# Attention scores as running sums over key differences, maxima bank by bank in the array's two halves, row sums folded by one transfer

## The chip, the cores and the metric

One core of a Trainium2 chip. Its engines are TensorE (PE, with its weight loads as PEld), VectorE (DVE), ScalarE (ACT), GpSimd (POOL) and SyncE (SP), which here issues the transfers. The metric is the device time of one execution in microseconds (us), lower is better.

## The reference

Two transformer layers over x of 32 batch elements x 100 rows x 256. Each adds a gated cross-attention over a context and a gated feed-forward part. The change is in the cross-attention of the second layer (L1): 16 heads, 100 queries, 1444 keys of 64 numbers that serve as values too.

```python
q_big = apply_rope(einsum('bshk,hkq->bshq', q_hk, w_kc_q))      # 192 per head
kv_r  = apply_rope(kv_c, sin_k, cos_k)                          # [32, 1444, 64]
scores = einsum('bhsr,bhlr->bhsl', q_r, k_r)                    # through W_qr, W_kr
attn   = softmax(scores)                                        # over 1444 keys
ctx_c  = einsum('bhsl,bld->bhsd', attn, kv_r)
x = x + tanh(g) * (einsum('bhsd,hkd->bhsk', ctx_c, w_kc_kv) -> [100, 2048]) @ Wo.T
```

The weights between queries and keys are multiplied together ahead, so that a query of a head is 64 numbers (`q1`, in `fp32r`, with its rounding remainder in `q2`), to be multiplied with the 64 of a rotated key (`k1`, with its remainder).

## The kernel before

The phase `phase_l1_attention` goes over 8 groups of 4 batch elements (G = 4). A group has a *head*, which makes the queries of its four elements for all 16 heads (wide matmuls L1431, rotation on DVE L1206 and POOL L1093, absorbed matmuls L1421, copies on ACT L1300), and then the four elements j = 0 to 3. An element has 1600 queries in two chunks of 800 (c = 0, 1, `CQS`); a chunk goes over its 1444 keys in 12 tiles of 121 or 120 keys (`NT`, `KP`). Two key tiles are a pair; the loop over pairs has for each key tile one *slot* (0 to 23 in an element) in which a job from `beside` may stand.

Order on PE in a pair: `scores` of both key tiles (per tile two halves of 400 queries, each half a matmul of `k1` with `q1`, L1476, and one of `k2` with `q2`, L1477, both over 128 rows: `k1` holds the keys rounded above and their remainder below, `q1` the queries twice, `k2` a row of ones and the rounded keys, `q2` the row of negative maxima and the query remainders); the job of the even slot; `values` of the pair before (L1490, exponentials times keys, two column halves); the job of the odd slot. ACT takes the exp of each half (L1350), POOL adds the two tiles of a pair (L1102), DVE adds these to the running sum (L1183, L1186). Scores use four PSUM banks in turn.

The softmax needs the maximum of each query ahead of its scores. `maxima` (L1394) multiplies 128 queries with all 1452 key columns into three banks `m_ps`: three matmuls over rows 0 to 63, 64 to 127 and 0 to 63; the seventh tile of a chunk has 32 queries and uses all 128 rows. DVE reduces the three banks at once (L1163) into `mneg`; PE waits for that before the next tile. SP carries each tile's column into a row of `q2` (L973). There are 14 tiles in an element, one to a job: those of chunk 0 in the element before (in the head for j = 0), those of chunk 1 in the element itself. Other jobs use the same banks: the key transposes (`turn_keys`, L1386), whose results ACT copies (L1306, L1312) and DVE splits (L1157); the sums over partitions (`sums`, L1401) and the output projection (`project`, L1407). The sums go through ACT (L1324), four transfers into `den`, a reciprocal on DVE (L1167), a transfer to HBM and two back into `rdb`, and the normalisation (L1171).

```python
FIRST, LATER, NEXT = (1, 2, 3, 4, 6, 7, 8), (0, 1, 3, 4, 6, 7, 8), (12, 13, 15, 16, 18, 19, 20)
v.tensor_reduce(mneg[0:n, c, t:t + 1], m_ps[0:n, :, 0:4 * KP], AX.XY, ALU.max, negate=True)
```

## Time and profile before

| | |
|---|---|
| median of 3 runs | 3444.43 us (3439.39 to 3446.43) |
| profiled execution | 3444.42 us, its span 3442.4 us |
| granted clock, mean | 0.944 of 2.4 GHz |
| PE busy | 3002.3 us, 87% |
| DVE busy | 2327.0 us, 68% |
| ACT, POOL busy | 1338.1 us (39%), 1559.6 us (45%) |

The span runs from the first to the last instruction. Matmuls overlap and their ends are modelled, so the cost of one is read from start to start. A row of a group gives busy time and mean duration, then the idle time of the engine before its instructions and what ended it.

### The profile page before, as it was taken

The numbers are of one execution on the slowest core, as the hardware profiler recorded it, in microseconds if no ns is written. First come the engines' busy times: TensorE is split into PE (matmuls) and PEld (weight loads), VectorE is DVE, ScalarE is ACT, GpSimd is POOL, SyncE is SP. The second block draws the span as 40 slices with busy tenths as digits, with TensorE's granted clock in tenths as the row PEclk, the third lists the DMA queues.
The fourth block names the chain that finished last, engine by engine and source line by source line (L and its number), as shares of the span: only waits on it lengthen the run. The fifth ranks groups of instructions, "written<-read, shape, count | busy, mean of one in ns | idle before, by whom it ended". The sixth has DMA issues, their size and how long they took to land. (4 is left out here: it accounts for less than half of the span.)

```text
span 3442.4 us, 55921 instructions
## 1 busy us (share of the span) xinstructions
PE 3002.3 (87%) x16656; PEld 2002.3 (58%) x16656; DVE 2327.0 (68%) x3226; ACT 1338.1 (39%) x2810; POOL 1559.6 (45%) x1035
## 2 busy tenths in 40 slices
PE   6999979999699999999999999999999999997344
PEld 4777779999555555565565565555556556554123
DVE  5777754544676676676676667658667667766787
ACT  1323322222244444434434444444443443443456
POOL 0000022222355555555565465556465556553566
PEclk9889979999799999999999999999999999999566
DMA  4000010000200000000000000000000000010100
GB/s 107 0 0 0 0 49 6 10 10 23 59 13 21 17 16 15 22 9 22 15 15 18 20 18 16 19 18 16 15 20 11 22 15 15 10 47 13 60 14 23
DMA packets 130212, 70.65 MB, mean 21 GB/s; under 512 B 83582, under 2 KB 124510, under 8 KB 129880
## 3 DMA queue, kind: packets, MB, share of 16 engines
q1 hardware_dynamic: 129944, 67.45, 7.8%
q8 instruction: 123, 2.02, 0.2%
q14 instruction: 145, 1.19, 0.1%
HBM read 56.95 MB, written 10.04 MB: 19 GB/s over the span
## 5 line engine op out<-in xcount | busy, mean ns | idle before, releaser
L1102 POOL TENSOR_TENSOR c_psum<-c_p 120x800 f32<-120x800 f32 (+1 forms) x384 | 750.8, 1961 | 779.0 <-ACT c_p L1350 463.7
L1163 DVE TENSOR_REDUCE c_mneg<-c_m_ps 128x1 fp32r<-128x1452 f32 (+1 forms) x448 | 744.8, 1662 | 412.6 <-PE c_m_ps L1394 412.4
L1350 ACT ACTIVATE c_p<-c_s_ps 120x400 f32<-120x400 f32 (+1 forms) x1536 | 655.2, 509 | 772.5 <-PE c_s_ps L1477 770.0
L1490 PE MATMUL c_o_ps<-c_p,c_val 120*64 120x400 f32 (+1 forms) x3072 | 598.8, 512 | 5.7 <-DVE c_q L1193 5.7
L1476 PE MATMUL c_s_ps<-c_q,c_k 128*120 128x400 f32 (+1 forms) x1536 | 569.3, 371 | 12.4 <-issue 5.7
L1477 PE MATMUL c_s_ps<-c_q,c_k 128*120 128x400 f32 (+1 forms) x1536 | 529.9, 345 | 0.0
L1394 PE MATMUL c_m_ps<-c_k,c_q 64*128 64x484 f32 (+1 forms) x1344 | 323.9, 439 | 99.9 <-DVE c_mneg L1163 70.8
L1476 PEld LDWEIGHTS c_s_ps<-c_q,c_k 128*120 128x120 f32 (+1 forms) x1536 | 278.9, 182 | 171.6 <-issue 158.8
L1093 POOL TENSOR_TENSOR l_rr<-c_psum,l_rr 96x400 f32<-96x400 f32 x256 | 260.8, 1040 | 210.7 <-DVE l_rr L1206 210.6
L1490 PEld LDWEIGHTS c_o_ps<-c_p,c_val 120*64 120x64 f32 (+1 forms) x3072 | 187.0, 136 | 281.2 <-issue 139.0
L1431 PE MATMUL c_s_ps<-c_xt,l_a 128*96 128x400 f32 x1536 | 309.5, 351 | 1.9 <-DVE c_xt L1151 1.9
L1394 PEld LDWEIGHTS c_m_ps<-c_k,c_q 64*128 64x128 f32 (+1 forms) x1344 | 129.5, 173 | 309.3 <-DVE c_mneg L1163 199.7
L1186 DVE TENSOR_TENSOR c_acc<-c_acc,c_psum 120x800 f32<-120x800 f32 x256 | 279.7, 1092 | 20.8 <-POOL c_psum L1102 18.3
L1431 PEld LDWEIGHTS c_s_ps<-c_xt,l_a 128*96 128x96 f32 x1536 | 240.1, 162 | 79.5 <-issue 41.3
L1477 PEld LDWEIGHTS c_s_ps<-c_q,c_k 128*120 128x120 f32 (+1 forms) x1536 | 280.3, 182 | 2.7
L1300 ACT ACTIVATE c_q<-c_o_ps 64x400 fp32r<-64x400 f32 x256 | 127.7, 499 | 262.6 <-PE c_o_ps L1421 257.9
L528 POOL TENSOR_TENSOR b_act_lo<-b_act,b_act_hi 128x400 fp32r<-128x400 f32 x88 | 91.9, 1049 | 292.4 <-ACT b_act_hi L672 292.4
L717 PE MATMUL b_gu_ps<-b_xt,l_a 128*128 128x400 f32 x1056 | 211.5, 352 | 9.3 <-DVE b_gated L563 9.3
L717 PEld LDWEIGHTS b_gu_ps<-b_xt,l_a 128*128 128x128 f32 x1056 | 193.5, 192 | 13.8 <-DVE b_gated L563 13.7
L1861 PE MATMUL d_y_ps<-d_w,d_hqt 128*128 128x256 bf16 x200 | 43.1, 390 | 110.9 <-ACT d_hqt L1810 110.9
L1206 DVE TENSOR_TENSOR c_psum<-c_s_ps,c_qcos 96x800 f32<-96x800 f32 x128 | 125.8, 983 | 17.8 <-PE c_s_ps L1431 15.6
L734 PE MATMUL b_y_ps<-b_wd,b_act_hi 128*100 128x256 f32 x704 | 129.2, 283 | 0.0
(232 smaller groups left out, 4157.4 us busy)
## 6 DMA issues: line engine op xcount, KB each, us to landing
c_rdb<-l_denominators SPq DMA_DIRECT2D x128, 100.0 KB, 2.7
c_kv<-in_ctx SPq DMA_DIRECT2D x32, 360.0 KB
c_q<-c_mneg SPq DMA_DIRECT2D x384, 0.5 KB, 1.9
c_den<-c_oden SPq DMA_DIRECT2D x256, 0.8 KB
x_rows<-in_x SPq DMA_DIRECT2D x4, 800.0 KB
x_spill<-x_rows SPq DMA_DIRECT2D x8, 400.0 KB
l_xa<-x_spill SPq DMA_DIRECT2D x8, 400.0 KB
c_xr<-x_spill SPq DMA_DIRECT2D x32, 100.0 KB
```

The source lines that it names most:

```text
L717: mm = pe.matmul(gu_ps[:, t % 2, j, 0:T], w[wi][:, k, t * 128:(t + 1) * 128], xt[x][:, k, :], start=(i == 0 and k == 0), stop=(i == 2 and ...
L734: mm = pe.matmul(y_ps[0:S, b // 2, (b % 2) * D:(b % 2 + 1) * D], rows[:, t % RING, b * S:(b + 1) * S], wd[w][:, t, :], start=(t == 0 and b ...
L1093: g.tensor_tensor(rot[:, i % 4, a, :], psum[0:HALF, i % 2, a * T:(a + 1) * T], rs[:, i % 2, (1 - a) * T:(2 - a) * T], ALU.add).then_inc(ro ...
L1102: g.tensor_tensor(psum[0:k, u % 2, :], p[0:k, 2 * u % 4, :], p[0:k, (2 * u + 1) % 4, :], ALU.add).then_inc(psum_ready, 1)
L1163: v.tensor_reduce(mneg[0:n, c, t:t + 1], m_ps[0:n, :, 0:4 * KP], AX.XY, ALU.max, negate=True).then_inc(mneg_ready, 1)
L1186: v.tensor_tensor(acc[0:k, :], acc[0:k, :], psum[0:k, q % 2, :], ALU.add).then_inc(acc_ready, 1)
L1350: a.activation(p[0:k, w % 4, i * HALFQ:(i + 1) * HALFQ], s_ps[0:k, (2 * w + i) % 4, 0:HALFQ], ACT.Exp).then_inc(exp_ready, 1)
L1394: mm = pe.matmul(m_ps[0:n, k, 0:4 * KP], q1[rows, j, c * CQS + t * 128:c * CQS + t * 128 + n], keys[j % 2][rows, k * 4 * KP:(k + 1) * 4 * ...
L1431: mm = pe.matmul(wide_banks(i)[0:HALF, a, 0:T], m.a[w][:, k, HEADS[i], a * HALF:(a + 1) * HALF], xt[x][:, k, :], start=(q == 0 and k == 0) ...
L1476: pe.matmul(o, k1[j % 2][:, r * KP:r * KP + k], q1[:, j, cols], start=True, stop=False)
L1477: mm = pe.matmul(o, k2[j % 2][:, r * KP:r * KP + k], q2[:, j, cols], start=False, stop=True)
L1490: mm = pe.matmul(o_ps[i * DL:(i + 1) * DL, 0:HALFQ], val[0:k, j % 2, r, :], p[0:k, w % 4, i * HALFQ:(i + 1) * HALFQ], start=(r == 0), stop ...
```

## The change

- **Scores.** The four PSUM banks are no longer begun anew for each key tile. Key tile r adds (k_r - k_(r-2)) times the queries onto what the bank holds of tile r - 2. Only tiles 0 and 1 of a chunk start a bank, with the row of negative maxima (`mrow`, against `first`, a row of ones). Queries of the first 400 columns lie in rows 0 to 63 and those of the second 400 in rows 64 to 127, so each matmul covers 64 rows; per key tile there are six, in pairs of the two halves: k1 with q1, k2 (the remainders) with q1, k1 with q2.
- **Keys.** ACT copies the transposed keys once unrounded (`kd`) and once rounded for maxima (`kmax`), DVE rounds the other parts (`round_keys`); POOL takes the differences in place (`difference`, five per element); ACT and DVE round and split them (`round_steps`, nine on ACT, `split_keys`, three on DVE).
- **Maxima.** 13 tiles of 128 queries go over both chunks. Each is three units, one per bank, with a matmul in alternating halves and a DVE reduction of its own (of 484 columns) (`reduce_unit`); seven small reductions per element combine them. In the head the seven tiles keep one reduction over three banks. `UNIT_SLOTS` places 43, 41, 41 and 10 units in the elements j = 0 to 3; the unit's matmul waits for the reduction that last read its bank. In the slots of the key transposes (9, 8, 7) and the one behind them, in slot 3 (j > 0) and in slot 15 there are no units.
- **Sums.** One transfer folds them in place of four, one spreads the inverses in place of two; sums stand in slots 3 and 15, projection in 15, reciprocal and normalisation one pair later.
- **Others.** One exp of a single element ahead of each group; `m.spare` reuses seven semaphores.

```diff
+        m.spare = [a_mm, a_hi, a_out, m_mm, m_out, c_mm, c_out]
...
+    NMT = -(-CH * CQS // 128)
+    NC0 = -(-CQS // 128)
+    starts = [min(128 * t, CH * CQS - 128) for t in range(NMT)]
+    NMU = 3 * NMT
+    NMG = G * NMU
+    COMBINED = {5: (0, 2), 11: (2, 4), 17: (4, 6), 20: (6, 7), 26: (7, 9), 32: (9, 11), 38: (11, 13)}
+    NCB = len(COMBINED)
+    GCB = G * NCB - 4
...
+        kd = sb("c_kd", [DL, NT * KP])
+        kmax = sb("c_kmax", [128, 2, 4 * KP], F32R)
+        klow, khigh = kmax[0:DL], kmax[DL:128]
+        mrow, first = sb("c_mrow", [128, CH, HALFQ], F32R), sb("c_first", [128, KP], F32R)
+        mneg, mpart = sb("c_mneg", [128, NMT], F32R), sb("c_mpart", [128, NMT, 3])
...
+        KEYS = {0: 9, 1: 8, 2: 7}
...
+        def tile_units(tiles):
+            for t in tiles[::2]:
+                yield from ((t, 0, 0), (t, 1, 1), (t, 2, 0))
+                if t + 1 in tiles:
+                    yield from ((t + 1, 1, 1), (t + 1, 0, 0), (t + 1, 2, 1))
+
+        UNITS = [*tile_units(range(NC0)), *tile_units(range(NC0, NMT))]
+        UNIT_SLOTS = ({**dict.fromkeys((1, 2, 3, 4, 5, 6, 11, 12, 13, 14, 16, 17, 18, 19, 20, 22, 23), 2), 7: 3, 8: 3, 21: 3},
+                      {**dict.fromkeys((0, 1, 2, 4, 5, 6, 7, 10, 11, 12, 13, 14, 16, 17, 18, 19, 21, 22, 23), 2), 20: 3},
+                      {**dict.fromkeys((0, 1, 2, 4, 5, 6, 9, 10, 11, 12, 13, 14, 16, 17, 18, 20, 21, 22, 23), 2), 19: 3},
+                      dict.fromkeys((0, 1, 2, 4, 5), 2))
...
+        HEAD_STEPS = {10: (0, 1), 11: (2,), 12: (3,), 13: (4, 5), 15: (6, 7, 8)}
+        TILE_STEPS = {15: (0,), 16: (1,), 17: (2,), 18: (3,), 19: (4,), 20: (5,), 21: (6,), 23: (7,)}
...
+                    sp.dma_start(den[:], oden[0:128:32, :].rearrange("o (p f) -> o p f", p=S // 4)).then_inc(den_loaded, 16)
...
+                    sp.dma_start(rdb[:], io["den"].rearrange("(i n) -> i n", i=2).unsqueeze(1).broadcast_to((2, DL, HALFQ))).then_inc(rdb_loaded, 16)
...
+                def load_tile(t):
+                    for i in range(2 * CH):
+                        lo, hi = max(128 * t, i * HALFQ), min(128 * t + 128, (i + 1) * HALFQ)
+                        if lo < hi:
+                            sp.dma_start(mrow[i % 2 * DL:i % 2 * DL + 1, i // 2, lo - i * HALFQ:hi - i * HALFQ].bitcast(F32),
...
+                                         mneg[lo - starts[t]:hi - starts[t], t:t + 1].bitcast(F32)).then_inc(row_loaded[i // 2], 16)
...
+                def difference(b, r):
+                    if r == NT - 2:
+                        g.wait_ge(kf_ready, PRIMED + (b + 1) * 3)
+                    else:
+                        g.wait_ge(kd_ready, PRIMED + b * 5 + (NT - 2 - r) // 2)
+                    g.sem_inc(m.carrier, 1)
+                    new, old = slice(r * KP, (r + 2) * KP), slice((r - 2) * KP, r * KP)
+                    g.tensor_tensor(kd[:, new], kd[:, new], kd[:, old], ALU.subtract).then_inc(kd_ready, 1)
...
+                        if j + 1 < G and at in (5, 6):
+                            for r in ((10, 8, 6), (4, 2))[at - 5]:
+                                difference(b + 1, r)
...
+                def round_keys(b):
+                    v.wait_ge(kf_ready, PRIMED + b * 3 + 1)
+                    v.tensor_copy(klow[:, 0, :], m_ps[0:DL, 0, 0:4 * KP]).then_inc(kmax_low, 1)
+                    v.wait_ge(kmax_high, PRIMED + b * 2 + 2)
+                    v.tensor_copy(klow[:, 1, :], m_ps[0:DL, 2, 0:4 * KP]).then_inc(kmax_low, 1)
+
+                def split_keys(b, j, pieces):
+                    for k in pieces:
                         cols = slice(k * 4 * KP, (k + 1) * 4 * KP)
-                        v.wait_ge(k1_hi, PRIMED + b * 3 + k + 1)
-                        v.tensor_tensor(k1[j % 2][DL:128, cols], m_ps[0:DL, k, 0:4 * KP], k1[j % 2][0:DL, cols].bitcast(F32),
+                        v.wait_ge(k1_hi, PRIMED + b * 6 + k + 1)
+                        v.sem_inc(m.carrier, 1)
+                        v.tensor_tensor(k2[j % 2][0:DL, cols], kd[:, cols], k1[j % 2][0:DL, cols].bitcast(F32),
                                         ALU.subtract).then_inc(k1_ready, 1)
 
-                def reduce_max(ch, c, t):
-                    n = QT[t]
-                    v.wait_ge(maxs_ready, PRIMED + ch * NQT + t + 1)
-                    v.tensor_reduce(mneg[0:n, c, t:t + 1], m_ps[0:n, :, 0:4 * KP], AX.XY, ALU.max, negate=True).then_inc(mneg_ready, 1)
+                def reduce_tile(gi, t):
+                    v.wait_ge(maxs_ready, PRIMED + gi * NMG + 3 * t + 3)
+                    v.tensor_reduce(mneg[:, t:t + 1], m_ps[:, :, 0:4 * KP], AX.XY, ALU.max, negate=True).then_inc(mpart_ready, 3)
+
+                def reduce_unit(it, n):
+                    t, bank, half = UNITS[n % NMU]
+                    v.wait_ge(maxs_ready, PRIMED + it * NMG + n + 1)
+                    v.tensor_reduce(mpart[:, t, bank:bank + 1], m_ps[:, bank, 0:4 * KP], AX.X, ALU.max, negate=True).then_inc(mpart_ready, 1)
+                    if n % NMU in COMBINED:
+                        tiles = slice(*COMBINED[n % NMU])
+                        v.wait_ge(mpart_ready, PRIMED + it * NMG + n + 1)
+                        v.tensor_reduce(mneg[:, tiles], mpart[:, tiles, :], AX.X, ALU.min).then_inc(mneg_ready, 1)
...
+                        if (j, c) != (0, 0) and q == 5:
+                            normalise(ch - 1, 1 - c)
+                        if j + 1 < G and c == 1 and q >= 3:
+                            split_keys(it * G + j + 1, j + 1, [q - 3])
...
+                def copy_keys(b):
                     for k in range(3):
                         a.wait_ge(kt_ready, PRIMED + b * 3 + k + 1)
-                        a.activation(k1[j % 2][0:DL, k * 4 * KP:(k + 1) * 4 * KP], m_ps[0:DL, k, 0:4 * KP], ACT.Copy).then_inc(k1_hi, 1)
-
-                def place_keys(b, j, k):
-                    cols = slice(k * 4 * KP, (k + 1) * 4 * KP)
-                    a.wait_ge(k1_hi, PRIMED + b * 3 + k + 1)
-                    a.sem_inc(m.carrier, 1)
-                    a.activation(k2[j % 2][DL:128, cols], k1[j % 2][0:DL, cols].bitcast(F32), ACT.Copy).then_inc(k2_ready, 1)
+                        a.activation(kd[:, k * 4 * KP:(k + 1) * 4 * KP], m_ps[0:DL, k, 0:4 * KP], ACT.Copy).then_inc(kf_ready, 1)
+                        if k > 0:
+                            a.activation(khigh[:, k - 1, :], m_ps[0:DL, k, 0:4 * KP], ACT.Copy).then_inc(kmax_high, 1)
+
+                def round_steps(b, j, n):
+                    cols = slice(n % 3 * 4 * KP, (n % 3 + 1) * 4 * KP)
+                    if n < 6:
+                        a.wait_ge(kd_ready, PRIMED + (b + 1) * 5)
+                        a.sem_inc(m.carrier, 1)
+                        a.activation(k1[j % 2][n // 3 * DL:(n // 3 + 1) * DL, cols], kd[:, cols], ACT.Copy).then_inc(k1_hi, 1)
+                    else:
+                        a.wait_ge(k1_ready, PRIMED + b * 3 + n - 5)
+                        a.sem_inc(m.carrier, 1)
+                        a.activation(k2[j % 2][DL:128, cols], k2[j % 2][0:DL, cols].bitcast(F32), ACT.Copy).then_inc(k2_ready, 1)
...
+                    a.activation(warm[:], m.ident[0:1, 0:1], ACT.Exp)
...
+                def maxima_unit(it, n):
+                    j, k = divmod(n, NMU)
+                    t, bank, half = UNITS[k]
+                    rows, q = slice(half * DL, (half + 1) * DL), slice(starts[t], starts[t] + 128)
...
+                    pe.wait_ge(mpart_ready, PRIMED + it * NMG + last_in(bank, n) + 1)
+                    pe.matmul(m_ps[:, bank, 0:4 * KP], q1[rows, j, q], kmax[rows, bank // 2 if half == 0 else bank - 1, :],
+                              start=True, stop=True).then_inc(maxs_ready, 1)
...
+                        bank = [s_ps[:, (2 * w + i) % 4, 0:HALFQ] for i in range(2)]
+                        if (j, c) == (0, 0) and r < 2:
+                            pe.wait_ge(roped, PRIMED + 2 * (it * H + H - 1 + r))
+                        if w >= 2:
+                            pe.wait_ge(exp_ready, PRIMED + 2 * it * NU + 2 * w - 2)
...
+                        if r < 2:
+                            for i in range(2):
+                                pe.matmul(bank[i][0:KP], first[side[i], :], mrow[side[i], c, :], start=True, stop=False, skip_group_check=True)
                         for i in range(2):
-                            at = 2 * w + i
-                            if at >= 4:
-                                pe.wait_ge(exp_ready, PRIMED + 2 * it * NU + at - 3)
-                            cols = slice(c * CQS + i * HALFQ, c * CQS + (i + 1) * HALFQ)
-                            o = s_ps[0:k, at % 4, 0:HALFQ]
-                            pe.matmul(o, k1[j % 2][:, r * KP:r * KP + k], q1[:, j, cols], start=True, stop=False)
-                            mm = pe.matmul(o, k2[j % 2][:, r * KP:r * KP + k], q2[:, j, cols], start=False, stop=True)
-                            mm.then_inc(s_ready, 1)
+                            pe.matmul(bank[i][0:k], k1[j % 2][side[i], keys], q1[side[i], j, q[i]], start=False, stop=False, skip_group_check=True)
+                        for i in range(2):
+                            pe.matmul(bank[i][0:k], k2[j % 2][side[i], keys], q1[side[i], j, q[i]], start=False, stop=False, skip_group_check=True)
+                        for i in range(2):
+                            pe.matmul(bank[i][0:k], k1[j % 2][side[i], keys], q2[side[i], j, c, :], start=False, stop=True, skip_group_check=True).then_inc(s_ready, 1)
```

## Rows read from the trace of the kernel before

**Rows 1.** The page: busy time of each engine, and TensorE's granted clock in 40 slices.
```profile
PE 3002.3 (87%) x16656; PEld 2002.3 (58%) x16656; DVE 2327.0 (68%) x3226; ACT 1338.1 (39%) x2810; POOL 1559.6 (45%) x1035
...
PEclk9889979999799999999999999999999999999566
```

**Rows 2.** Busy time by stretch: one group's head, elements 0, 1 and 3.
```profile
core 0: us, PE busy (x) PEld busy (x) DVE busy (x) ACT busy (x) POOL busy (x), PEclk, DMA share, GB/s
2037.28:2097.83 60.55, 57.92 (x307) 39.33 (x306) 53.09 (x60) 17.89 (x36) 33.65 (x33) 1.00 0.03 5
2097.83:2153.01 55.18, 49.47 (x254) 27.63 (x255) 36.99 (x30) 27.68 (x61) 29.42 (x17) 1.00 0.10 24
2153.01:2211.08 58.07, 53.26 (x279) 30.45 (x279) 37.66 (x32) 25.38 (x58) 31.11 (x18) 1.00 0.08 18
...
2269.10:2319.27 50.17, 49.07 (x263) 28.53 (x261) 30.00 (x39) 22.03 (x52) 34.09 (x19) 1.00 0.09 21
```

**Rows 3.** Timeline of PE, one engine, in the second half of an element.
```profile
start us, us, engine line op out<-in xcount [idle before <-releaser]
...
2002.05 0.70 PE L1394 MATMUL c_m_ps<-c_k,c_q 64*128 64x484 f32 x3
2002.68 1.56 PE L1490 MATMUL c_o_ps<-c_p,c_val 120*64 120x400 f32 x8
...
2007.08 0.84 PE L1394 MATMUL c_m_ps<-c_k,c_q 128*32 128x484 f32 x3 [0.22 <-DVE c_mneg L1163]
2007.85 1.56 PE L1490 MATMUL c_o_ps<-c_p,c_val 120*64 120x400 f32 x8
2009.34 0.45 PE L1476 MATMUL c_s_ps<-c_q,c_k 128*120 128x400 f32 x1
2009.63 0.35 PE L1477 MATMUL c_s_ps<-c_q,c_k 128*120 128x400 f32 x1
...
2011.00 1.56 PE L1490 MATMUL c_o_ps<-c_p,c_val 120*64 120x400 f32 x8
2012.49 3.70 PE L1407 MATMUL c_m_ps<-l_cvo,c_ct 128*100 128x256 f32 x16
2015.84 0.53 PE L1476 MATMUL c_s_ps<-c_q,c_k 128*121 128x400 f32 x1
...
2020.70 0.55 PE L1401 MATMUL c_m_ps<-c_acc,c_ones 121*32 121x200 f32 x8
2021.18 1.56 PE L1490 MATMUL c_o_ps<-c_p,c_val 121*64 121x400 f32 x8
```

**Rows 4.** Timeline of PE and its loads, 2157.110 to 2157.118; one block of loads.
```profile
2157.11 0.49 PE L1394 MATMUL c_m_ps<-c_k,c_q 64*128 64x484 f32 x2 [0.27 <-DVE c_mneg L1163]
...
2157.11 0.19 PEld L1394 LDWEIGHTS c_m_ps<-c_k,c_q 64*128 64x128 f32 x2 [0.96 <-DVE c_mneg L1163]
...
2004.51 0.30 PEld L1394 LDWEIGHTS c_m_ps<-c_k,c_q 64*128 64x128 f32 x3 [0.96 <-DVE c_mneg L1163]
```

**Rows 5.** Timeline of DVE in the stretch of element 1.
```profile
2155.39 1.67 DVE L1163 TENSOR_REDUCE c_mneg<-c_m_ps 128x1 fp32r<-128x1452 f32 x1 [2.55 <-PE c_m_ps L1394]
2156.97 0.98 DVE L1186 TENSOR_TENSOR c_acc<-c_acc,c_psum 120x800 f32<-120x800 f32 x1
2157.87 1.66 DVE L1163 TENSOR_REDUCE c_mneg<-c_m_ps 128x1 fp32r<-128x1452 f32 x1
...
2167.35 0.20 DVE L1167 RECIPROCAL c_rden<-c_den 100x8 f32<-100x8 f32 x1
...
2172.81 1.66 DVE L1171 TENSOR_TENSOR c_ct<-c_onum,c_rdb 128x400 f32<-128x400 f32 x1
```

**Rows 6.** Groups by line in the stretch of element 1: DVE, ACT, POOL.
```profile
L1157 DVE TENSOR_TENSOR c_k<-c_m_ps,c_k 64x484 fp32r<-64x484 f32 x3 | 1.8, 647 | 0.5 <-ACT c_k L1306 0.5
...
L1350 ACT ACTIVATE c_p<-c_s_ps 120x400 f32<-120x400 f32 (+1 forms) x48 | 20.5, 509 | 26.4 <-PE c_s_ps L1477 26.3
...
L1312 ACT ACTIVATE c_k<-c_k 64x484 fp32r<-64x484 f32 x3 | 1.8, 604 | 0.1
...
L1102 POOL TENSOR_TENSOR c_psum<-c_p 120x800 f32<-120x800 f32 (+1 forms) x13 | 25.9, 1997 | 30.0 <-ACT c_p L1350 16.3 <-DVE c_acc L1186 13.7
```

**Rows 7.** Timeline of PE: the first score matmul of element 1.
```profile
2153.01 0.44 PE L1476 MATMUL c_s_ps<-c_q,c_k 128*121 128x400 f32 x1 [0.68 <-DMA c_q<-c_mneg]
```

More of the change, by code:

```diff
@@ new lines, in units_at, with last_in, first_in @@
+        def units_at(j, slot):
+            first = 3 * NC0 + sum(sum(UNIT_SLOTS[i].values()) for i in range(j)) + sum(n for s, n in UNIT_SLOTS[j].items() if s < slot)
+            return range(first, first + UNIT_SLOTS[j].get(slot, 0))
+        assert units_at(G - 1, CT).start == NMG
+        assert all(units_at(j, KEYS[j]).start == NMU * (j + 1) for j in KEYS)
+        def last_in(bank, n):
+            return next(i for i in range(n - 1, -1, -1) if UNITS[i % NMU][1] == bank)
+        def first_in(bank, n):
+            return next(i for i in range(n, n + NMU) if UNITS[i % NMU][1] == bank)
@@ L938, in _ @@
             def _(sp):
+                for c in m.spare:
+                    sp.sem_clear(c)
                 for c in counters:
@@ L1533, in group @@
+                        for n in units_at(j, slot):
+                            maxima_unit(it, n)
                     for u, j, c, q in pairs():
@@ L1572, in count @@
         def count(name):
-            counters.append(sem(name))
+            counters.append(m.spare.pop() if m.spare else sem(name))
             return counters[-1]
```

283 lines of the change are left out of this document (149 added, 134 removed).

## Prediction

> **What bounds the kernel now.** I began with the page: TensorE (PE) is busy 87% of the span, VectorE (DVE) 68%, and PE's clock is granted at its upper level (2.4 GHz) nearly everywhere [rows 1]. All edits but a list of spare semaphores lie in the attention of the second layer, which fills some 2256 us (8 x 282.0, below). I cut one of its eight groups into its head and its four batch elements, each stretch from its first matmul to that of the next [rows 2] (the fourth is not shown; it repeats the third in 58.0 us). The five take 60.6, 55.2, 58.1, 58.0 and 50.2 us, 282.0 together, and the groups repeat this within half a microsecond. The reader is to see that in the heads DVE is busy 53 of 60.6 us, and in the elements PE 49 to 53 us, DVE 30 to 38.
>
> What an element costs PE is read from start to start in the timeline, since the ends are modelled [rows 3]. A pair of key tiles has a block of 8 score matmuls, 1.66 us from its start to that of what follows: 8 x 0.183, and 0.19 for entering and leaving (the first interval is 0.28, the later ones 0.18). The values take 1.49, a maximum of one query tile 0.63 (0.77 for the 32-row tile), the output projection 3.35, the sums 0.48, the key transposes about 1.2. For the third stretch: 12 x (1.66 + 1.49) + 12 x 0.63 + 2 x 0.77 + 3.35 + 2 x 0.48 + 1.2 = 52.4. It takes 58.1: 5.7 us are waits, nearly all for the maximum on DVE, before the next tile may overwrite the three banks. The same sum gives 50.1, 52.4 and 47.4 for the other three, so waits of 5.1, 5.6 and 2.8.
>
> **The change, part by part.**
>
> *Scores.* Four matmuls per key tile over 128 rows become six over 64 rows, three in each half of the array, issued in pairs with different halves and banks. What a pair costs is shown by the maxima, whose first two matmuls are such a pair: both loads and both matmuls start inside one window of 8 ns [rows 4], and the block of three takes 0.63, where three over 128 rows take 0.77 [rows 3]. So I price a pair like one matmul, 0.183. A block falls to 6 x 0.183 + 0.19 = 1.29. The two blocks of an element in which a chunk begins have two pairs more for the row of maxima, +0.37 each. So 12 x 1.29 + 0.74 = 16.2 us where 12 x 1.66 = 19.9 stood. The trace does not show pair after pair, so both ends: below, 0.183 (the same 400 columns stream); then 0.21, if the two loads of a pair take turns (the first interval shows a load of 120 columns uncovered for 0.10); then 0.283, if no load is covered; above, 0.366, if the halves take turns. I take the lower end, because the row with two starts is the same form of matmul.
>
> *A rule weighed.* In the maxima the third load belongs to the half in which the first matmul still streams, and the three loads are over 0.30 us after the block began [rows 4]: a load and a matmul of one half do overlap. The Trainium skill (TensorE: Matmul & The Clock Gate, Part 3) says that a weight load overlaps a running matmul only when its row group differs. By that rule each pair would start 0.10 later and the time would be 3377; by the row it is 3233.
>
> *Maxima.* Instead of 14 blocks of three matmuls there are 39 single ones per element, two or three to a slot, halves alternating, so a slot costs PE one step of 0.22 (0.63 less the 0.19, halved) and no entry, as the scores beside it use the same halves. Stretch by stretch (43, 41, 41 and 10 units): 23, 21, 21 and 5 steps, 5.2, 4.7, 4.7 and 1.1 us.
>
> PE's floor: third and fourth stretch 16.2 + 17.9 + 4.7 + 3.35 + 0.96 + 1.2 = 44.3; second 16.2 + 17.9 + 5.2 + 0.5 + 1.2 + 1.5 (the last query pair) = 42.5; fifth 16.2 + 17.9 + 1.1 + 3.35 + 0.96 + 0.7 (turning rows) = 40.2.
>
> *DVE.* Its maximum over 1452 elements takes 1.58 from start to start, the sum over 800 takes 0.90 [rows 5]. That is 1.04 ns per element, so 484 elements take 0.57, and three of them 1.71 instead of 1.58. Bounds: 0.50 (the slope alone) and 0.65 (the busy time of the form with 484 columns [rows 6]). Third stretch: 41 x 0.57 = 23.4; seven small minima that each wait for the maximum just issued, 0.25 each (nearest row the reciprocal, 0.20 [rows 5], and a lost overlap), 1.8; twelve running sums 11.5; two normalisations 2.1; reciprocals and residual 0.6; two copies of keys 1.1; three subtractions 1.9. Together 42.4, beside PE's 44.3.
>
> These don't simply overlap. PE can be ahead by three banks only, and gives DVE no maxima in slots 8, 9, 3 and 15. DVE then runs dry: around the projection PE spends 1.49 + 0.48 + 3.35 + 1.29 = 6.6 us between two slots, for which DVE has 2.5 (4.1 idle); around the other sums 3.3 for 2.1 (1.1 idle); around the keys 5.6 for 3.2 (2.4 idle). 42.4 + 7.6 = 50.0. In the dense slots between, four maxima and a running sum are 3.2 to 3.5 us of DVE, with key subtractions and normalisations up to 4.3, against PE's 1.29 + 1.49 + 0.44 = 3.2: there DVE leads. With 1 us for a bank that comes round after two units, 51.0 for the third and fourth stretch. Second: 43.1 us of DVE, 5.5 idle: 49.0. Fifth: PE's 40.2, and 3 for the backlog and the chunk's row: 43.0.
>
> *Head.* Seven tiles keep the wide maximum. DVE gets two key copies and keeps three subtractions, two operations more, +1.1: 61.6. The exp of one element placed ahead of the group takes a table load off ACT; I count nothing, as PE there has other work.
>
> *ACT and GpSimd (POOL).* ACT gets 8 more copies of 484 columns per element, 0.56 to 0.60 each, some 4.8 us, hidden by the 26 us in which it waits for scores [rows 6]; uncovered they would cost 150 us. POOL gets five subtractions over 242 columns, from 2.00 us for 800 some 0.6 each, 3 us, in 30 us of waits [rows 6]; with them its share rises, and DVE's operations without PSUM may stretch, as the normalisation did that took 1.66 us [rows 5]. For that I put 0 to 2 us per element into the range.
>
> *Transfers.* SP issues 16 row pieces instead of 14, one fold instead of four, one spread instead of two. They lie beside PE work except the row before an element's first score, 0.68 us late at 2153.01 [rows 7]. In the second stretch it is reduced later (slot 21), 1 us, which is in the waits.
>
> **Sum.** 61.6 + 49.0 + 51.0 + 51.0 + 43.0 = 255.6, less than 282.0 by 26.4; x 8 = 211. The profiled execution took 3444.42 us (span 3442.4), equal to the median of the runs. 3444.4 - 211 = 3233.
>
> **Rivals.**
>
> *PE sets the pace.* If DVE's units cost 0.50 and its sequences interleave well, each element stands 2 us above its floor: 61.6 + 44.5 + 46.3 + 46.3 + 42 = 240.7, x 8 = -330, 3114. Against it: DVE then still has 39 us of work and 7 of holes. 0.10.
>
> *DVE costs more.* Units at 0.65 (135 per group outside the head, x 0.08 = 11) and 1 to 2 us per element from POOL: 255.6 + 15 = 271, 3356; or ACT's copies hold up the exponentials with the like result. 0.15.
>
> *Loads uncovered.* Pair interval 0.283: floors rise by 12 x 6.2 x 0.1 = 7.4 to 50 to 52 us, PE leads, with 3 us of waits 61.6 + 53 + 55 + 55 + 49 = 273.6: 3377. 0.06.
>
> *The halves take turns (the other side).* Interval 0.366: a score block costs 12 x 0.183 + 0.19 = 2.39, the maxima 0.22 a unit; floors 61 to 64, fifth 56, group about 308: 3444 + 8 x 26 = 3652. With waits of 3 us per element over the floors the group comes to 282 at an interval of about 0.31; from there on the change loses. Against it are the two starts in 8 ns; for it, that they don't accumulate and that no second pair follows. 0.06.
>
> *No net change* within 0.2% (7 us, about what a measurement of this kernel can tell): interval near 0.30. 0.01.
>
> **Chances.** Forecast 0.62, the others as above: faster 0.93, same 0.01, slower 0.06. Range 3150 to 3340: from between the first rival and the forecast (two thirds of DVE's lower bound) to most of the second.
>
> **What would show it.** The 12 matmuls of two key tiles should stand in six steps of 0.18, pairs a few ns apart. The DVE rows of 484 elements should be 0.65 busy, 0.57 apart. PE's waits should be for them in slots 16 to 23 and before the key transposes. The stretches should read 62, 49, 51, 51, 43. Wrong would be: pairs further apart than 0.2, exponentials waiting on ACT's copies or POOL, a row that arrives late by several us, or a lower granted clock.

## The result, and the profile after

The kernel after takes 3499.36 us, the median of 4 runs (3484.78 to 3511.37), beside 3445.43 (3439.39 to 3449.17) for the one before on the same chip. The ratio is 1.0156, 95% interval 1.0112 to 1.0201: slower by 54 us, where 3233, 211 us faster, was forecast. The profiled execution took 3511.37 us (span 3509.6, mean clock 0.911 where it had been 0.944).

From the page of the kernel after: span, busy times, granted clock and two groups of DVE (busy and mean, then idle before and releaser).

```profile
span 3509.6 us, 61563 instructions
...
PE 2942.7 (84%) x18344; PEld 1971.0 (56%) x18352; DVE 2449.7 (70%) x4170; ACT 1488.0 (42%) x3074; POOL 1640.1 (47%) x1196
...
PEclk9888879999899998999999999899999999998566
...
L1283 DVE TENSOR_TENSOR c_acc<-c_acc,c_psum 120x800 f32<-120x800 f32 x256 | 322.4, 1259 | 63.8 <-POOL c_psum L1178 61.8
...
L1268 DVE TENSOR_TENSOR c_ct<-c_onum,c_rdb 128x400 f32<-128x400 f32 x64 | 37.4, 585 | 153.4 <-DMA c_rdb<-l_denominators 153.3
```

PE is busy for 59.6 us less than before [rows 1], with 1,688 matmuls more: the scores did get cheaper. But its share of the span fell from 87 to 84%, and the normalisation of DVE waited 153.3 us for the transfer `c_rdb`, the spread of the inverses.

The same cut of a group as in [rows 2], now with all five stretches (head, then elements 0 to 3), of the kernel after:

```profile
core 0: us, PE busy (x) PEld busy (x) DVE busy (x) ACT busy (x) POOL busy (x), PEclk, DMA share, GB/s
2071.00:2134.60 63.60, 58.32 (x309) 39.36 (x307) 54.44 (x63) 23.49 (x45) 36.24 (x38) 1.00 0.04 9
2134.60:2185.60 51.00, 46.60 (x315) 26.37 (x317) 40.19 (x65) 30.66 (x69) 34.27 (x22) 0.97 0.10 21
2185.60:2250.30 64.70, 53.39 (x335) 30.86 (x333) 43.66 (x69) 30.24 (x66) 33.58 (x22) 0.89 0.10 16
2250.30:2311.30 61.00, 52.92 (x337) 30.43 (x333) 40.24 (x69) 30.34 (x66) 33.82 (x22) 0.92 0.10 18
2311.30:2361.00 49.70, 45.04 (x307) 25.08 (x307) 33.00 (x48) 22.54 (x53) 31.74 (x19) 0.97 0.12 22
sum 290.00, PE 256.27 PEld 152.09 DVE 211.52 ACT 137.27 POOL 169.65; mean PE 51.25 PEld 30.42 DVE 42.30 ACT 27.45 POOL 33.93
```

Forecast were 61.6, 49, 51, 51 and 43, together 255.6. It is 290.0, 34.4 more, and 8 x 34.4 = 275 of the 278 us by which the profiled execution missed. Element 0, with one normalisation where the others have two, is 2 us over; elements 1 and 2 are 13.7 and 10.0 over, at a clock of 0.89 and 0.92, and element 3 is 6.7 over.

The largest single loss, from the timeline of the kernel after at the start of element 1 (SP's issues are SPq; the bracket is the idle time of the engine and what ended it):

```profile
2183.30 0.52 SPq L1005 DMA_DIRECT2D l_denominators<-c_rden  x1
...
2184.81 0.58 SPq L1010 DMA_DIRECT2D c_rdb<-l_denominators  x1
...
2192.04 0.58 DVE L1268 TENSOR_TENSOR c_ct<-c_onum,c_rdb 128x400 f32<-128x400 f32 x1 [5.28 <-DMA c_rdb<-l_denominators]
2192.53 0.65 DVE L1246 TENSOR_TENSOR c_k<-c_kd,c_k 64x484 fp32r<-64x484 f32 x1
2193.10 1.22 DVE L1256 TENSOR_REDUCE c_mpart<-c_m_ps 128x1 f32<-128x484 f32 x2
...
2193.80 0.85 PE L1530 MATMUL c_m_ps<-c_kmax,c_q 64*128 64x484 f32 x2 [5.08 <-DVE c_mpart L1256]
...
2194.35 0.16 DVE L1260 TENSOR_REDUCE c_mneg<-c_mpart 128x2 fp32r<-128x6 f32 x1
2194.56 0.99 DVE L1283 TENSOR_TENSOR c_acc<-c_acc,c_psum 120x800 f32<-120x800 f32 x1
```

In the program the normalisation stands ahead of the next maxima, and DVE takes them in that order: it begins the normalisation 7.2 us after the spread was issued and the maxima behind it, at 2193.10. Until then PE has no bank for its next maxima and idles for 5.08 us. In the kernel before, the transfers of the same place were issued at 2168.89, and the normalisation began at 2172.81 without idle time, right behind a maximum [rows 5].

PE then pays a second time, by its clock. Windows of the kernel after, same columns as above:

```profile
2185.50:2188.00 2.50, 2.50 (x24) 1.81 (x24) 1.25 (x3) 1.60 (x4) 0.00 (x0) 1.00 0.14 32
2188.00:2193.50 5.50, 0.72 (x6) 0.03 (x2) 1.46 (x3) 0.09 (x1) 0.00 (x0) 0.85 0.08 26
2193.50:2199.50 6.00, 5.70 (x24) 3.52 (x24) 4.34 (x8) 2.91 (x6) 3.77 (x3) 0.57 0.03 2
2199.50:2205.00 5.50, 5.31 (x47) 3.25 (x45) 3.35 (x6) 2.87 (x8) 4.33 (x3) 1.00 0.01 0
```

At work again, PE runs 6 us at a granted clock of 0.57, most of them at its lower level (1.2 of 2.4 GHz): 24 matmuls, of mixed forms, in 6.0 us, and 47 in the next 5.5. Such a wait of 5.2 to 5.7 us comes once in each of the eight groups, and in all eight the 6 us from the normalisation on show a clock of 0.50 to 0.52. The other waits of the stage are at most 3.5 us. In the heads DVE waits 3.2 to 3.4 us for the same transfer, but PE has work meanwhile and its clock stays 1.00. In element 2 DVE waits 1.9 and 2.7 us for it, PE is idle for 2.1 and 2.4, and the clock falls to 0.57 and 0.50 again. Over the whole attention stage the clock is 0.95, where it was 1.00 before. The waiting line of `c_rdb` names the first loss only: over the stage PE is busy for 2033.6 of 2316 us here and for 1975.1 of 2178 us in the kernel of experiment 1, with the same matmuls. So some 58 of the 138 us between the two stages are the same work done more slowly, an estimate from these busy times.

The score blocks themselves did what was forecast. PE's timeline of the kernel after, a block of two key tiles:

```profile
2199.98 0.44 PE L1619 MATMUL c_s_ps<-c_q,c_k 64*120 64x400 f32 x2
2200.26 0.34 PE L1621 MATMUL c_s_ps<-c_q,c_k 64*120 64x400 f32 x2
2200.44 0.34 PE L1623 MATMUL c_s_ps<-c_q,c_k 64*120 64x400 f32 x2
2200.63 0.34 PE L1619 MATMUL c_s_ps<-c_q,c_k 64*120 64x400 f32 x2
2200.81 0.35 PE L1621 MATMUL c_s_ps<-c_q,c_k 64*120 64x400 f32 x2
2200.99 0.35 PE L1623 MATMUL c_s_ps<-c_q,c_k 64*120 64x400 f32 x2
2201.17 0.38 PE L1530 MATMUL c_m_ps<-c_kmax,c_q 64*128 64x484 f32 x2
```

What counts are the starts: twelve matmuls stand in six steps of 0.18, the first a little longer, and the block takes 1.19 to the maxima behind it.

### The profile page after: what moved, and what is told of

It is laid out like the page before. It is cut to its first block and busy times, and to the rows that moved or that the text cites. A ratio compares the mean times of both kernels' runs of the same rounds, so it can differ in the third digit from the quotient of the medians.

```text
span 3509.6 us, 61563 instructions
## 1 busy us (share of the span) xinstructions
PE 2942.7 (84%) x18344; PEld 1971.0 (56%) x18352; DVE 2449.7 (70%) x4170; ACT 1488.0 (42%) x3074; POOL 1640.1 (47%) x1196
## 5 line engine op out<-in xcount | busy, mean ns | idle before, releaser
L1256 DVE TENSOR_REDUCE c_mpart<-c_m_ps 128x1 f32<-128x484 f32 x1080 | 656.5, 651 | 164.5 <-PE c_m_ps L1530 159.9
L1635 PE MATMUL c_o_ps<-c_p,c_val 120*64 120x400 f32 (+1 forms) x3072 | 629.2, 533 | 27.5 <-ACT c_onum L1429 16.3
L1530 PE MATMUL c_m_ps<-c_kmax,c_q 64*128 64x484 f32 x1080 | 340.8, 471 | 174.1 <-DVE c_mpart L1256 170.3
L1530 PEld LDWEIGHTS c_m_ps<-c_kmax,c_q 64*128 64x128 f32 x1080 | 153.2, 194 | 405.8 <-DVE c_mpart L1256 329.4
L1283 DVE TENSOR_TENSOR c_acc<-c_acc,c_psum 120x800 f32<-120x800 f32 x256 | 322.4, 1259 | 63.8 <-POOL c_psum L1178 61.8
L1635 PEld LDWEIGHTS c_o_ps<-c_p,c_val 120*64 120x64 f32 (+1 forms) x3072 | 194.4, 141 | 292.4 <-issue 170.1
L1619 PE MATMUL c_s_ps<-c_q,c_k 64*120 64x400 f32 (+1 forms) x1536 | 319.8, 375 | 2.3 <-ACT c_p L1462 2.3
L1623 PE MATMUL c_s_ps<-c_q,c_k 64*120 64x400 f32 (+1 forms) x1536 | 302.9, 355 | 0.0
L1621 PE MATMUL c_s_ps<-c_q,c_k 64*120 64x400 f32 (+1 forms) x1536 | 302.6, 355 | 0.0
L1619 PEld LDWEIGHTS c_s_ps<-c_q,c_k 64*120 64x120 f32 (+1 forms) x1536 | 165.0, 188 | 60.6 <-issue 32.1
L1621 PEld LDWEIGHTS c_s_ps<-c_q,c_k 64*120 64x120 f32 (+1 forms) x1536 | 172.3, 188 | 4.8
L1623 PEld LDWEIGHTS c_s_ps<-c_q,c_k 64*120 64x120 f32 (+1 forms) x1536 | 172.7, 188 | 0.9
L1268 DVE TENSOR_TENSOR c_ct<-c_onum,c_rdb 128x400 f32<-128x400 f32 x64 | 37.4, 585 | 153.4 <-DMA c_rdb<-l_denominators 153.3
```

Of the source, the lines that this page charges most:

```text
L1256: v.tensor_reduce(mpart[:, t, bank:bank + 1], m_ps[:, bank, 0:4 * KP], AX.X, ALU.max, negate=True).then_inc(mpart_ready, 1)
L1283: v.tensor_tensor(acc[0:k, :], acc[0:k, :], psum[0:k, q % 2, :], ALU.add).then_inc(acc_ready, 1)
L1530: pe.matmul(m_ps[:, bank, 0:4 * KP], q1[rows, j, q], kmax[rows, bank // 2 if half == 0 else bank - 1, :], start=True, stop=True).then_inc( ...
L1619: pe.matmul(bank[i][0:k], k1[j % 2][side[i], keys], q1[side[i], j, q[i]], start=False, stop=False, skip_group_check=True)
L1621: pe.matmul(bank[i][0:k], k2[j % 2][side[i], keys], q1[side[i], j, q[i]], start=False, stop=False, skip_group_check=True)
L1623: pe.matmul(bank[i][0:k], k1[j % 2][side[i], keys], q2[side[i], j, c, :], start=False, stop=True, skip_group_check=True).then_inc(s_ready, 1)
```

## The experiments

**1. Two transfers instead of one.** The kernel after with the spread of the kernel before:

```diff
-  sp.dma_start(rdb[:], io["den"].rearrange("(i n) -> i n", i=2).unsqueeze(1).broadcast_to((2, DL, HALFQ)))
+  for i in range(2):
+      sp.dma_start(rdb[i * DL:(i + 1) * DL, :], io["den"][i * HALFQ:(i + 1) * HALFQ].partition_broadcast(DL))
```

> The changed kernel with one edit undone: the inverses go back to all partitions by two transfers of 64 partitions, not by one of 128. Theory A (the one wide transfer lands 7.2 us after its issue, the two of before 2.7 us after; DVE stands at the normalisation for it, the maxima queue behind, PE idles and its clock falls): DVE's wait for this transfer falls from 153 us to under 40 us, the third and fourth stretch of a group from 65 and 60.5 us to about 57 and 55, the total to 3330 to 3390. Rival B (the order on SP's queue makes the transfer late, not its shape): the landing falls but the wait stays over 100 us, total over 3450. Rival C (DVE's maxima in single units and the paired matmuls are too dear): no change, 3480 or more.

3367.28 us (3361.0 to 3370.97), ratio to the kernel before 0.9773 (0.9741 to 0.9804): the sign of the whole change turns on this line. The same stretches of this kernel:

```profile
2004.50:2066.40 61.90, 58.17 (x309) 39.24 (x307) 55.71 (x63) 23.83 (x46) 36.59 (x38) 1.00 0.03 6
2066.40:2117.30 50.90, 45.20 (x312) 25.72 (x312) 40.31 (x64) 30.45 (x67) 34.06 (x22) 1.00 0.09 21
2117.30:2174.60 57.30, 49.10 (x335) 28.32 (x335) 43.61 (x69) 29.92 (x66) 33.70 (x22) 1.00 0.10 20
2174.60:2229.00 54.40, 48.97 (x335) 28.26 (x335) 42.42 (x69) 30.01 (x66) 34.44 (x22) 1.00 0.09 20
2229.00:2275.70 46.70, 42.89 (x308) 24.02 (x306) 34.22 (x50) 22.54 (x53) 33.22 (x19) 1.00 0.09 25
sum 271.20, PE 244.33 PEld 145.57 DVE 216.27 ACT 136.74 POOL 172.01; mean PE 48.87 PEld 29.11 DVE 43.25 ACT 27.35 POOL 34.40
```

The clock is 1.00 throughout this group (0.98 over the whole attention stage), and the wait for `c_rdb` is 17.4 us in 9 places. PE's wait for DVE's single maxima falls from 170.3 to 111.2 us. The group is 18.8 us shorter than after, and still 15.6 over the forecast.

**2. The same edit alone, on the kernel before.** The two transfers of the kernel before replaced by the single one, nothing else.

> The kernel before with this one edit alone: one transfer of 128 partitions in place of two of 64. Theory A: landing goes from 2.7 to about 7 us, up to 4.5 us more per chunk less the slack; DVE's wait for it goes from 40 us to 200 us or more, total 3445 plus 100 to 250. Rivals B and C: within 15 us of 3445.

3618.25 us (3611.97 to 3642.23), ratio 1.0522 (1.0468 to 1.0576). The tile view of `c_rdb` in this kernel (waits in us and times):

```profile
L965 SPq DMA_DIRECT2D c_rdb<-l_denominators x64: 570/583/601, 1015.7 to 3341.8; - x64
...
  DVE c_ct L1170: 259.8, 64
```

The edit costs 173 us here (3618 less 3445), more than in the kernel after (132), where nearly as many normalisations waited but for less: here 64 wait 4.1 us each, there 63 wait 2.4 each.

**3. Is it the number of transfers, or their description?** The single transfer differs from the pair in two things: it is one, and its source is described as two blocks of 64 copies. Two kernels part these. The first has two transfers of 64 rows, each described as two blocks of 32 copies (the inverses so reach other rows); the second has one transfer of 128 rows, described as one block (the second 400 queries of a chunk are divided by the sums of the first 400).

```diff
+  for i in range(2):                                             # first kernel
+      sp.dma_start(rdb[i * DL:(i + 1) * DL, :], io["den"].rearrange("(i n) -> i n", i=2).unsqueeze(1).broadcast_to((2, DL // 2, HALFQ)))
+  sp.dma_start(rdb[:], io["den"][0:HALFQ].partition_broadcast(2 * DL))   # second kernel
```

> The kernel after, with the spread as two transfers of 64 rows again, but each of them described like the single one: a source of two blocks, the rows 32 copies of each block. (The inverses so reach the wrong rows; which query is divided by which sum is changed, nothing else.) Theory A, the description of the transfer makes it slow (its outermost step has only two values, so that few DMA engines get work: the single transfer moved its 128 packets in 5.5 us at a DMA share of 0.14, the two transfers in 1.5 us at 0.43): the two transfers are as slow together as the single one, 128 packets in about 5.5 us, VectorE waits for c_rdb 130 to 170 us in total, and the time stays at 3470 to 3520, near the 3499 of the kernel after. Theory B, one transfer of 128 rows is slow because it is one: two transfers of 64 rows are fast whatever their description, the wait is 15 to 30 us and the time 3350 to 3385, as in the run with two transfers (3367). By the Trainium skill (DMA: Bandwidth & Descriptors, How many engines) a transfer runs on the largest number of DMA engines up to 16 that divides the slowest dimension of both sides, which is Theory A with two engines.

> The kernel after, with the spread as one transfer of 128 rows still, but of one block: all 128 rows get the first 400 inverses (the second half of a chunk's queries is divided by the sums of the first; the bytes moved and the packets are the same). Theory A, the description makes it slow: now its outermost step has 128 values, the 128 packets run in about 1.5 us, the landing is 2.5 to 3 us after the issue, VectorE's wait for c_rdb falls from 153 to 10 to 30 us, and the time is 3350 to 3385. Theory B, one transfer of 128 rows is slow because it is one: 5.5 us, a wait of about 150 and 3480 to 3520.

Two transfers of two blocks: 3527.02 us (3521.17 to 3535.42), ratio 1.0246 (1.0226 to 1.0266). One transfer of one block: 3363.07 us (3347.11 to 3366.93), ratio 0.9749 (0.972 to 0.9778). The second kernel's wait for `c_rdb` is 11.0 us in 9 places, and its transfer lands 3.0 us after the issue (median), where the pair lands after 2.7. It is the description, not the number. Windows in which the packets of one spread ran (the last two figures are DMA share and GB/s), in the kernel before, the kernel after, the first kernel and the second:

```profile
2170.24:2171.72 1.48, 1.36 (x7) 1.01 (x8) 1.48 (x3) 0.00 (x0) 1.48 (x2) 1.00 0.43 138
```

```profile
2186.17:2191.69 5.52, 2.56 (x20) 1.17 (x16) 0.58 (x2) 1.69 (x4) 0.00 (x0) 1.00 0.14 40
```

```profile
2184.70:2190.60 5.90, 2.59 (x20) 1.21 (x16) 0.59 (x2) 1.69 (x4) 0.00 (x0) 0.96 0.11 34
```

```profile
2105.90:2107.50 1.60, 1.60 (x18) 1.10 (x16) 0.73 (x2) 1.19 (x4) 0.00 (x0) 1.00 0.34 109
```

The same 128 packets of 1600 B keep 0.11 to 0.14 of the 16 DMA engines busy, about two engines (2 of 16 is 0.125), wherever the source has two blocks, and 0.43 and 0.34 where it has not (the fourth window holds some 174 of the 205 KB). The Trainium skill (DMA: Bandwidth & Descriptors, "Why a DMA increments its semaphore by 16 and not by 1") says that a transfer is split over the largest number of engines, up to 16, that divides the slowest dimension of both its sides. For the two-block source that is 2, and the shares agree; for 64 or 128 copies it is 16, and no view here shows how many engines took part in those. The first kernel is slower than the kernel after by 28 us; its waits for `c_rdb` are 176.7 us in 64 places, against 153.3 in 63.

**4. Order of the issues.** In the kernel after, SP writes and spreads the inverses of chunk 1 behind the row pieces of two more tiles. Here they go first, still as the single transfer:

```diff
+  write_inverses(b * CH)
+  spread_inverses(b * CH)
   ...                      # the row pieces of combinations 2 and 3
-  write_inverses(b * CH)
-  spread_inverses(b * CH)
```

> The changed kernel with the order on SP's queue alone changed: in the second half of an element the inverses are written and spread (by one transfer still) ahead of the last two loads of rows of maxima, not behind them. Theory A (the transfer's 7.2 us): the spread at the start of the third stretch is issued about 6 us earlier, so DVE's wait of 5.3 us there goes, but the wait of 2.2 us in the middle of an element stays: 153 us falls to some 80, total 3430 to 3470. Rival B (order): the whole wait goes, total under 3400. Rival C: no change.

3447.98 us (3428.81 to 3457.87, 10 runs), ratio 1.001 (0.999 to 1.0031); the wait for `c_rdb` is 87.0 us in 39 places. So the late issue was part of the stall. But the earlier issue has a price as well, since the loads of the rows of maxima now stand behind the slow transfer; the first score matmuls of a chunk wait for them, as this group of PE shows, where the kernel after has 1.3 us of such a wait in one place:

```profile
L1617 PE MATMUL c_s_ps<-c_mrow,c_first 64*121 64x400 f32 x256 | 53.1, 403 | 53.3 <-DMA c_mrow<-c_mneg 31.7 <-issue 10.6 <-ACT c_p L1462 7.7
```

With both edits:

> The changed kernel with both edits: two spreads, and inverses written and spread ahead of the last two row loads. After the two spreads alone DVE waits 17 us for the transfer and ACT 43 us for the normalised product before it may copy the next sums. If the order on SP's queue still costs, these fall and the time is 15 to 50 us under 3367; if it only moves the rows of maxima back, within 10 us of 3367 or above.

3350.75 us (3340.94 to 3358.87), ratio 0.9724 (0.9697 to 0.975), the wait 1.7 us in one place, and none for the rows of maxima; ACT's wait for the normalised product stays at 42.6 us. It is the best version with the whole computation, 93 us under the kernel before beside it (3443.5) and 149 under the one after. Once the transfer is quick, the order is worth only 17 us, with the slow one 51. Taken order by order, the slow transfer costs 132 us issued late (3499 less 3367) and 97 issued early (3448 less 3351).

**5. Do the halves really overlap?** The kernel of experiment 1 with all score matmuls on rows 0 to 63 (`side = (low, low)`; the scores of the second 400 queries are left out).

> Two spreads, and all score matmuls on rows 0 to 63: the same count, lengths and banks, but both halves of the queries take the lower half of the array (the second half's scores are left out, the lower rows' are computed for its columns). If the halves overlap in the kernel as changed, a block of two key tiles goes from 6 steps of 0.18 us to 12, 1.1 us more, 384 times: 420 us, less what of PE's waits for DVE it takes up: total 3600 to 3790. If the array worked them off in turn anyway: within 20 us of 3367.

3657.22 us (one run), 290 more than with both halves. The 420 us of longer blocks are partly taken up by PE's wait for DVE's single maxima, which falls from 111 to 28 us. Its PE timeline:

```profile
2306.04 0.52 PE L1620 MATMUL c_s_ps<-c_q,c_k 64*121 64x400 f32 x2
2306.41 0.52 PE L1622 MATMUL c_s_ps<-c_q,c_k 64*121 64x400 f32 x2
2306.77 0.52 PE L1624 MATMUL c_s_ps<-c_q,c_k 64*121 64x400 f32 x2
```

Two matmuls now take 0.36, one after the other, where a pair takes 0.18. This is what the rival in which the halves take turns described for the scores; the kernel after doesn't do it. That its price of 3652 lies so near is luck, since that sum let the maxima take turns too, which they don't do here.

**6. Pairs that are not neighbours.** In the kernel after, the two loops over halves are merged, so that the three matmuls of one half stand ahead of the three of the other.

```diff
-  for i in range(2):   (before each of the second and third matmul)
```

> The changed kernel with the six score matmuls of a key tile in another order: in the lower half k1 and k2, in the upper half k1 and k2, then the two last ones as before. If matmuls of different halves overlap and those of one half don't, a tile takes four steps of 0.18 us (low, low with nothing beside it, high, high, then the pair, the first of a half starting beside the last of the other: low, low+high, high, pair) instead of three, so a block of two tiles 8 x 0.183 + 0.09 in place of 1.1 to 1.2 us, about 0.36 us more. If the halves take turns anyway, the block already costs 12 steps and nothing changes.

The expectation describes another order than the one that ran, with the third matmul of both halves last; in the run all three of a half stood together. One run: 3493.18 us, within the 3484.78 to 3511.37 of the kernel after. Its PE timeline:

```profile
2314.65 0.45 PE L1619 MATMUL c_s_ps<-c_q,c_k 64*120 64x400 f32 x2
2314.93 0.35 PE L1620 MATMUL c_s_ps<-c_q,c_k 64*120 64x400 f32 x2
2315.12 0.35 PE L1621 MATMUL c_s_ps<-c_q,c_k 64*120 64x400 f32 x2
2315.30 0.35 PE L1619 MATMUL c_s_ps<-c_q,c_k 64*120 64x400 f32 x2
```

Still pairs, six steps of 0.18: the two matmuls of L1619, three instructions apart in the program, start 10 ns apart. Neither theory of the expectation held: the first wanted more time, and the second had no change, but for halves that take turns.

**7. What remains over the forecast.** Three kernels on top of experiment 1, each looked at once. The first halves DVE's single maxima (they read 242 of 484 columns), the second cuts POOL's key differences to one column (they are left out but for that), the third has POOL add 400 of 800 columns of each pair of exponentials (half of the softmax sums is left out; DVE's adds are unchanged).

```diff
-  v.tensor_reduce(mpart[...], m_ps[:, bank, 0:4 * KP], ...)
+  v.tensor_reduce(mpart[...], m_ps[:, bank, 0:2 * KP], ...)
```
```diff
-  new, old = slice(r * KP, (r + 2) * KP), slice((r - 2) * KP, r * KP)
+  new, old = slice(r * KP, r * KP + 1), slice((r - 2) * KP, (r - 2) * KP + 1)
```
```diff
-  g.tensor_tensor(psum[0:k, u % 2, :], p[0:k, 2 * u % 4, :], p[0:k, (2 * u + 1) % 4, :], ALU.add)
+  g.tensor_tensor(psum[0:k, u % 2, 0:HALFQ], p[0:k, 2 * u % 4, 0:HALFQ], p[0:k, (2 * u + 1) % 4, 0:HALFQ], ALU.add)
```

> Two spreads, and each single maximum on DVE reads 242 of its 484 columns (half of the keys' scores are left out of the maxima; matmuls stay whole). Theory D (after the transfer is mended DVE's maxima lead in the elements): 0.25 us less for each of 39, 10 us of DVE per element, the group falls from 271 towards PE's floor with waits of 3 us per element, 248, total about 3180. Rival P (other waits of PE lead: exponentials, POOL, rows): over 3320.

> Two spreads, and POOL's five subtractions of keys per element over one column instead of 242 (the key differences are left out). Theory D: POOL has slack, within 20 us of 3367. If POOL's part of the change leads (ACT waits 52 us for the differences, DVE's sums stretch beside them): 40 us or more under it.

> Two spreads, and POOL's sum of two key tiles over 400 of 800 columns (half of the softmax sums are left out), with the other half set once. POOL is busy about 1 us less per pair. If DVE's running sums are stretched by POOL's work beside them (mean 1.26 us where an undisturbed one takes 0.98), their mean falls to 1.0 to 1.1 and the total by 50 to 100 us, to about 3290. If they are not, they stay at 1.26 and the total within 20 us of 3367, less what DVE waits for POOL (62 us in all).

They took 3279.14, 3351.93 and 3264.41 us (one run each) against 3367.28: 88, 15 and 103 less. The first lies between the two theories of its expectation, the second is within the 20 us that slack allows, the third is a little beyond the gain expected if POOL stretches DVE's sums. Groups by line of the kernel of experiment 1, and then of the one with half the pair sums:

```profile
L1179 POOL TENSOR_TENSOR c_psum<-c_p 120x800 f32<-120x800 f32 (+1 forms) x384 | 745.4, 1944 | 601.1 <-ACT c_p L1463 320.8 <-DVE c_acc L1284 144.9 <-DVE c_acc L1281 132.1
L1463 ACT ACTIVATE c_p<-c_s_ps 120x400 f32<-120x400 f32 (+1 forms) x1536 | 657.4, 508 | 463.4 <-PE c_s_ps L1624 410.8 <-POOL c_psum L1179 50.2
...
L1284 DVE TENSOR_TENSOR c_acc<-c_acc,c_psum 120x800 f32<-120x800 f32 x256 | 323.7, 1265 | 63.8 <-POOL c_psum L1179 61.7
```

```profile
L1465 ACT ACTIVATE c_p<-c_s_ps 120x400 f32<-120x400 f32 (+1 forms) x1536 | 657.8, 508 | 461.6 <-PE c_s_ps L1626 444.8 <-POOL c_psum L1179 14.7
...
L1179 POOL TENSOR_TENSOR c_psum<-c_p 120x400 f32<-120x400 f32 (+1 forms) x384 | 437.3, 1139 | 841.3 <-ACT c_p L1465 476.2 <-DVE c_acc L1282 205.1 <-DVE c_acc L1285 159.9
...
L1285 DVE TENSOR_TENSOR c_acc<-c_acc,c_psum 120x800 f32<-120x800 f32 x256 | 285.5, 1115 | 54.6 <-POOL c_psum L1179 52.2
```

With less on POOL, the same DVE add takes 1.115 instead of 1.265, ACT waits for POOL's buffers 14.7 us instead of 50.2, and DVE for its sums 52.2 instead of 61.7. PE's wait for DVE's single maxima falls from 111.2 to 62.6 us with half the columns on DVE and to 67.4 with half the sums on POOL, so both edits shorten the same wait in the main. No run has both, so it isn't shown what they give together, and each run leaves out work that the result needs. The key differences have slack. How much of the 103 us is the stretched DVE work and how much the waits, these runs don't part.

**8. The other merged transfer.** The kernel before with one fold transfer in place of four.

```diff
-  for i in range(4):
-      sp.dma_start(den[i * S // 4:(i + 1) * S // 4, :], oden[32 * i:32 * i + 1, :].rearrange("o (p f) -> o p f", p=S // 4))
+  sp.dma_start(den[:], oden[0:128:32, :].rearrange("o (p f) -> o p f", p=S // 4))
```

> The kernel before with the row sums folded by one transfer instead of four, nothing else. DVE waits 35 us there for the fold in all; SP issues three transfers of 0.7 us less per chunk. If a single transfer of 100 pieces is no slower to land than the last of four: 5 to 35 us faster, 3410 to 3440. If it is slow as the single spread was (5.5 us for 128 pieces against 1.5): slower by up to 100 us.

3441.97 us (3432.03 to 3451.97), ratio 1.0003 (0.999 to 1.0017): no change in time, though DVE's wait for the fold, 34.8 us in 26 places before, is gone. That wait cost nothing where it stood. Of two merged transfers of the change one is free and one cost 132 us.

## Why the prediction was wrong, point by point

- **Transfers: this step failed.** "SP issues ... one spread instead of two. They lie beside PE work" priced the new transfer at nothing and gave it no range and no rival. It took 5.5 us for its packets instead of 1.5, 7.2 from issue to use, and it does not lie beside work: DVE meets it in program order. Undoing it gives 132 us of the 266 by which the median missed (3499 less 3233). The trace of the kernel before has the rows that show the risk, in its tile view of `c_rdb`, and the prediction has none of them (waits in us and times, then the landing):

```profile
  DVE c_ct L1171: 40.0, 19
...
DMA to landing us min/median/max: 2.6/2.7/4.0
```

DVE waited for this transfer 19 times already, 40.0 us in all, with two transfers that landed in 2.7 us. A hidden transfer with a margin near nothing has to be priced like a new instruction, and so has a description that the trace doesn't show.
- **The rule weighed** was the wrong one to look for. Loads of one half do run while that half streams: the score blocks keep 0.18 per pair, with no 0.10 between. By the Trainium skill's rule (TensorE: Matmul & The Clock Gate, Part 3) the time would have been 3377 for another reason; the trace after does not agree with it, and the 3367 of experiment 1 lies near that only by chance. The rule that spoke against this change was the one on DMA engines of experiment 3.
- **Scores: right.** Priced 0.183 a pair and 1.29 a block; read 0.18 and six steps. One half alone makes it 0.36 (experiment 5).
- **Maxima and DVE's units: right in size.** 0.651 busy where 0.65 was said, and back to back 0.57 to 0.58 (two in 1.21 or 1.22); the small minima cost more than priced. One is busy for only 0.16, but it also waits for the maximum before it to end: from the start at which the next operation could stand, 2193.10 + 1.14, to the 2194.56 at which it does are 0.32, where 0.25 was priced, some 0.5 us per element more.
- **Head: right.** 61.9 with two transfers for 61.6.
- **Element times: the second term that was mis-sized.** With two transfers the elements take 50.9, 57.3, 54.4 and 46.7 where 49, 51, 51 and 43 were said: 15.3 a group, 122 us. In element 1 DVE's busy time is 43.6 where 42.4 was summed, in element 2 it is 42.4. So its work was summed nearly right, though with errors of both signs: a running sum is busy for 1.26, where in the kernel before it was for 1.09 and 0.96 from start to start was priced, a split for 0.86 instead of 0.63, while a normalisation takes 0.60 in element 1 instead of 1.05. What is off is its idle time, 57.3 less 43.6 and 54.4 less 42.4, 13.7 and 12.0 us, where 7.6 and 1 were put. The holes around projection and keys were close (5.1 and 2.7 in element 1, 4.1 and 2.4 priced); what was missed is that a late POOL sum or a stretched DVE operation next to a hole isn't made good, since PE is at most three banks ahead. The forecast kept 0 to 2 us per element for that and put none of it in the sum. That mechanism is read from the waits, not tried by itself; experiment 7 shows two levers (POOL's sums 103 us, DVE's maxima 88), not the exact split.
- **ACT and POOL: mostly hidden**, as said: ACT still waits 410.8 us for scores with two transfers, and the differences are worth at most 15 us. POOL's old work, not its new work, was what stood in the way. In one place it isn't hidden, and the forecast has no term for that: the key transposes, in slot 9 of every element before, stand in slot 7 of element 2 now, and PE waits there for POOL's rotated keys (`c_kva`), 2.3 us once in each group; in the kernel before it never waited for them. The group of PE in the kernel after:

```profile
L1500 PE MATMUL c_m_ps<-ident,c_kva 121*64 121x121 f32 x384 | 50.7, 288 | 22.8 <-POOL c_kva L1144 18.0 <-DVE c_mpart L1256 4.4 <-issue 0.4
```

With two transfers the wait is still 17.9 us, with half the pair sums on POOL 5.3. No run moves the slot alone.
- **The clock: named at the end, never priced.** It fell, to 0.57 for 6 us behind the stall at the start of element 1, and with the transfer quick it is 1.00 in the same stretches, so it came with PE's idle time. By PE's busy time it is some 58 us of what the slow transfer cost. With two transfers 0.98 is left over the attention stage, behind PE's shorter waits for banks, where before it was 1.00: of PE's 1975 busy us there, 2% are at most some 40 us of the 134 over the forecast (3367 less 3233), estimated from these figures and not tried by itself.
- **The rivals.** 3356 ("DVE costs more") is near the 3367 with two transfers, in part for a cause of that kind. None named a transfer, so the range of 3150 to 3340 excluded the result.

## What to carry to other kernels

Merging transfers changes more than their number: look at the outermost step of both sides, since a broadcast written as two blocks ran on about two of 16 DMA engines and took 5.5 us where the same bytes took 1.5. Before a transfer is called hidden, find the instruction that uses it, what is queued behind that on its engine, and how much margin the rows of before show; here it was already waited for. When the next engine is nearly as busy as the leading one (here PE for 87% of the span and DVE for 68 before, 86 and 74 with two transfers), a saving on the leading one is worth only what the next ones leave: of 26 us a group that the sums promised, 11 came (282.0 to 271.2).
